# Image 0 of an eight-image kernel: two of the four directional convolutions on TensorE instead of one

## What is computed

```
def _L0_conv_ref(x, w_h, w_v, w_d45, w_d135, w_att1, w_att2, w_proj):
    feat_h = _dwconv(x, w_h, ((0, 0), (3, 3)))                 # direction 0
    feat_v = _dwconv(x, w_v, ((3, 3), (0, 0)))                 # direction 1
    feat_d45 = _dwconv(x, w_d45 * diag, ((3, 3), (3, 3)))      # direction 2
    feat_d135 = _dwconv(x, w_d135 * anti, ((3, 3), (3, 3)))    # direction 3
    feats = jnp.stack([feat_h, feat_v, feat_d45, feat_d135], axis=1)
    context = jnp.mean(feats * feats, axis=(3, 4)).reshape(x.shape[0], -1)
    hid = jax.nn.leaky_relu(context @ w_att1.T, negative_slope=0.2)
    attn = softmax over the four directions of (hid @ w_att2.T)
    feat_geom = jnp.sum(attn * feats, axis=1)
    return lax.conv_general_dilated(feat_geom, w_proj, (1, 1), ((1, 1), (1, 1)), ...)
x = x + _L0_conv_ref(_gn(x), ...)
x = x + _L1_conv_ref(_gn(x), ...)
```

## Time and profile before

| | |
|---|---|
| time of three runs | 3992.3, 3993.53, 4000.81 us; median 3993.53 |
| span of the profiled execution, first to last instruction | 4000.2 us |
| mean granted clock of TensorE | 0.963 |
| busy: PE, DVE, ACT | 93%, 76%, 41% of the span |
| L790, the start of image 0's attention | at 232.74 us |

### The profile page before, as it was taken

The page is one execution under the profiler, slowest core; times in us unless marked ns, Lnnn a source line. Parts: engine busy times, 40 slices in busy tenths (PEclk is TensorE's granted clock), DMA queues, the critical chain, the costliest instruction groups (busy, mean ns, idle before and its releaser), DMA issues.

```text
span 4000.2 us, 56479 instructions
## 1 busy us (share of the span) xinstructions
PE 3726.0 (93%) x21202; PEld 3089.2 (77%) x21202; DVE 3030.3 (76%) x2829; ACT 1624.1 (41%) x2912; POOL 210.4 (5%) x376
## 2 busy tenths in 40 slices
PE   4659999999999999999999999999999999999998
PEld 2347788968799687977889687996879778896977
DVE  7987978789777898679787897788986797853020
ACT  3412662237522564126622375225641266212430
POOL 1001000100001000010001000010000000010000
PEclk8879999999999999999999999999999999999999
DMA  4354222823156221732228221562217322260002
GB/s 111 99 148 106 64 63 43 216 63 76 35 120 171 55 67 39 175 99 64 63 44 214 63 76 37 120 169 57 66 39 177 96 65 63 46 166 27 1 7 30
DMA packets 164716, 344.11 MB, mean 86 GB/s; under 512 B 110336, under 2 KB 110576, under 8 KB 164432
## 3 DMA queue, kind: packets, MB, share of 16 engines
q1 hardware_dynamic: 141392, 255.36, 25.9%
q0 software_dynamic: 23040, 84.95, 9.6%
HBM read 189.27 MB, written 150.99 MB: 85 GB/s over the span
## 4 chain that ended last, share of the span: by engine, by line
PE 81%; DVE 10%; issue 5%; ACT 3%; DMA 1%; POOL 0%; SPq 0%; DVEq 0%; ACTq 0%; POOLq 0%
PE banks L936 15%; PE banks L937 15%; PE banks L942 15%; PE banks L951 7%; PE banks L974 6%; PE banks L1003 6%; PE banks L961 6%; DVE feat L702 5%; PE banks L1013 3%; PE banks L967 3%; PE banks L968 3%; DVE e_lo L725 2%; PE banks L990 1%; DMA feat<-feats_d 1%; ACT z L529 1%
## 5 line engine op out<-in xcount | busy, mean ns | idle before, releaser
L702 DVE SCALAR_TENSOR_TENSOR feat<-xin,w,feat 96x1536 f32<-96x1536 f32 x540 | 943.5, 1809 | 1.1
L936 PE MATMUL banks<-e_hi,a_hi 96*96 96x384 f32 x1728 | 597.6, 346 | 40.9 <-ACT a_hi L572 40.9
L936 PE MATMUL banks<-e_hi,wp_hi 96*96 96x384 f32 x1728 | 587.8, 341 | 22.5 <-DVE e_lo L828 11.5
L937 PE MATMUL banks<-e_lo,a_hi 96*96 96x384 f32 x1728 | 595.2, 345 | 0.0
L937 PE MATMUL banks<-e_lo,wp_hi 96*96 96x384 f32 x1728 | 586.8, 340 | 0.0
L702 DVE SCALAR_TENSOR_TENSOR feat<-xin,wh,feat 96x1536 f32<-96x1536 f32 x288 | 520.8, 1808 | 53.5 <-ACT feat L488 52.7
L702 DVE SCALAR_TENSOR_TENSOR feat<-xin,wv,feat 96x1536 f32<-96x1536 f32 x288 | 521.0, 1809 | 8.9 <-ACT feat L488 8.9
L500 ACT ACTIVATE sqjunk<-feat 96x1536 bf16<-96x1536 f32 x192 | 284.3, 1481 | 231.9 <-DVE feat L702 228.4
L563 ACT ACTIVATE res<-banks 96x768 f32<-96x768 f32 x96 | 77.6, 808 | 728.2 <-PE banks L942 728.2
L936 PEld LDWEIGHTS banks<-e_hi,a_hi 96*96 96x96 f32 x1728 | 287.0, 166 | 74.1 <-issue 35.0
L961 PEld LDWEIGHTS banks<-mats,z 96*96 96x96 f32 x3072 | 294.7, 168 | 60.6 <-issue 46.8
(11 more groups left out here) (145 smaller groups left out, 4844.9 us busy)
## 6 DMA issues: line engine op xcount, KB each, us to landing
feats_d<-feat SPq DMA_DIRECT2D x160, 576.0 KB, 4.1
feat<-feats_d SPq DMA_DIRECT2D x160, 576.0 KB, 6.7
feat<-in_x SPq DMA_DIRECT2D x48, 576.0 KB, 6.9
res<-in_x POOLq DMA_DIRECT2D x96, 288.0 KB, 4.0
out<-x POOLq DMA_DIRECT2D x96, 288.0 KB, 2.8
out<-res POOLq DMA_DIRECT2D x96, 288.0 KB, 4.4
xin<-in_x SPq DMA_DIRECT2D x32, 792.0 KB, 8.7
xin<-in_x SPq DMA_DIRECT2D x16, 684.0 KB, 10.3
```

The source lines that it names most:

```text
L702: dve.scalar_tensor_tensor(out=dst, in0=src, scalar=taps_w[d](k), in1=dst, op0=ALU.mult, op1=ALU.add).then_inc(tap_done, 1)
L936: pe.matmul(dst, whi[:, t, :], rows(e_hi, a0, n, dx), start=(t == CENTRE_FIRST[0]), stop=False)
L937: pe.matmul(dst, whi[:, t, :], rows(e_lo, a0, n, dx), start=False, stop=False)
```

## The change

For image 0 TensorE makes directions 1 and 3 (`BY_PE`), VectorE directions 0 and 2. A second set of seven diagonals, `v_diag`, is laid into a part of `x1` that is not yet in use, and ScalarE fills it ahead of `bk`. The semaphores `last_dir_sums` and `last_dir_made` become `pe_dir_sums` and `pe_dir_made`, which count halves of both directions in TensorE's order (`pe_halves`); the counts of VectorE's taps and ScalarE's first taps are adapted. ScalarE's order for image 0 changes: within a unit's work, the square of the second direction moves behind the normalisation and the first tap of the unit after next, and ahead of the copies out of PSUM; in `start`, both first taps come ahead of the copies. All other images are as before.

```diff
+BY_PE = (1, 3)
+def by_pe(b, d):
+    return first_image(b) and d in BY_PE
+def pe_halves(q, d):
+    return 2 * (q * len(BY_PE) + BY_PE.index(d))
...
+        v_diag = x1[0:C, 0:KT * C].rearrange("p (t c) -> p t c", c=C)
...
                 if first_image(b) and q >= 2:
-                    sp.wait_ge(last_dir_sums, 2 * (q - 1))
+                    sp.wait_ge(pe_dir_sums, pe_halves(q - 1, BY_PE[0]))
...
-                        if first_image(b) and d == DIRS - 1:
-                            sp.wait_ge(last_dir_made, 2 * (q + 1))
+                        if by_pe(b, d):
+                            sp.wait_ge(pe_dir_made, pe_halves(q, d) + 2)
...
             for k in range(KT):
+                act.activation(v_diag[:, k, :], ident, ACT.Identity, scale=wv[:, k:k + 1]).then_inc(diag_ready, 1)
+            for k in range(KT):
                 act.activation(bk[:, k, :], ident, ACT.Identity,
...
-                if by_pe:
+                if by_pe(b, d):
                     for half in range(2):
-                        act.wait_ge(last_dir_sums, 2 * q + half + 1)
+                        act.wait_ge(pe_dir_sums, pe_halves(q, d) + half + 1)
...
                 if u + 2 < UNITS:
                     work += [(first_tap, u + 2, 0), (first_tap, u + 2, 1)]
+                if first_image(b):
+                    work.append(work.pop(1))
+                    if u + 2 < UNITS:
+                        work[-2:] = work[:-3:-1]
...
-                for u in range(2):
-                    first_tap(b, u, 0)
-                    first_tap(b, u, 1)
+                order = [(0, 0), (1, 0), (0, 1), (1, 1)] if first_image(b) else [(0, 0), (0, 1), (1, 0), (1, 1)]
+                for u, d in order:
+                    first_tap(b, u, d)
...
-                    dirs = [d for d in dirs if d < DIRS - 1]
+                    dirs = [d for d in dirs if d not in BY_PE]
...
                     if first_image(b):
-                        dve.wait_ge(last_dir_sums, LEAD)
+                        dve.wait_ge(pe_dir_sums, pe_halves(LEAD // 2, BY_PE[0]))
                     edge_rows(b, NCH - 1)
...
-            def last_direction():
-                pe.wait_ge(diag_ready, KT)
+            def pe_directions():
+                pe.wait_ge(diag_ready, len(BY_PE) * KT)
                 for q in range(NCH):
                     pe.wait_ge(xin_ready, q + 1)
                     if q == 0 or q == NCH - 1:
                         pe.wait_ge(edge_zero, 1 if q == 0 else EDGES)
+                    for d, diag in zip(BY_PE, (v_diag, bk)):
+                        for half in range(2):
+                            before = pe_halves(q, d) + half - 2
+                            if before >= 0:
+                                pe.wait_ge(pe_dir_made, before + 1)
+                            for h in range(2):
+                                for k in range(KT):
+                                    dy, dx = tap_shift(d, k)
+                                    r0 = PAD + dy + (2 * half + h) * TR
+                                    last = pe.matmul(conv_ps[0:C, half, h, 0:TR * W], diag[:, k, :],
+                                                     xin[:, q % 2, r0:r0 + TR, PAD + dx:PAD + dx + W],
+                                                     start=(k == 0), stop=(k == KT - 1))
+                            last.then_inc(pe_dir_sums, 1)
```

More of the change, by code:

```diff
@@ L103, in taps_before @@
 def taps_before(b):
-    return 0 if first_image(b) else b * (NCH * TAPS) - NCH * (KT - 1)
+    return 0 if first_image(b) else b * (NCH * TAPS) - NCH * len(BY_PE) * (KT - 1)
+def by_pe(b, d):
+    return first_image(b) and d in BY_PE
+def pe_halves(q, d):
+    return 2 * (q * len(BY_PE) + BY_PE.index(d))
 def unit_taps(b, u, k, parity):
[L110 to L113, removed]
+    if first_image(b):
+        return taps_before(b) + u * (KT - 1) + k
+    return taps_before(b) + u // 2 * TAPS + u % 2 * (TAPS // 2) + 2 * (k - 1) + parity + 1
 def firsts_before(b, q):
-    return q * (DIRS - 1) if first_image(b) else b * (DIRS * NCH) - NCH + q * DIRS
+    left = DIRS - len(BY_PE)
+    return q * left if first_image(b) else b * (DIRS * NCH) - len(BY_PE) * NCH + q * DIRS
 def tap_shift(d, k):
@@ L216, in build @@
         tap_done = sem("tap_done")
-        last_dir_sums, last_dir_made = sem("last_dir_sums"), sem("last_dir_made")
+        pe_dir_sums, pe_dir_made = sem("pe_dir_sums"), sem("pe_dir_made")
         diag_ready = sem("diag_ready")
@@ L324, in load_xin @@
                 else:
-                    last_turn = TAPS - (KT - 1) if isinstance(b, int) and b == 1 else TAPS
+                    last_turn = TAPS - len(BY_PE) * (KT - 1) if isinstance(b, int) and b == 1 else TAPS
                     wait(sp, tap_done, 0 if first_image(b) else taps_before(b) + (q - 1) * last_turn)
                 if first_image(b) and q >= 2:
-                    sp.wait_ge(last_dir_sums, 2 * (q - 1))
+                    sp.wait_ge(pe_dir_sums, pe_halves(q - 1, BY_PE[0]))
                 apart(sp)
                 if isinstance(b, int) and b == 1:
-                    sp.wait_ge(last_dir_sums, 2 * NCH)
+                    sp.wait_ge(pe_dir_sums, pe_halves(NCH, BY_PE[0]))
                 if isinstance(b, int) and b == 0 and q < 2:
@@ L474, in first_tap @@
                 dy, dx = tap_shift(d, 0)
-                by_pe = first_image(b) and d == DIRS - 1
                 act.wait_ge(xin_ready, b * NCH + q + 1)
@@ L481, in first_tap @@
                     act.wait_ge(feat_stored[d], (b * (NCH - 1) + q) * 16)
-                if by_pe:
+                if by_pe(b, d):
                     for half in range(2):
-                        act.wait_ge(last_dir_sums, 2 * q + half + 1)
+                        act.wait_ge(pe_dir_sums, pe_halves(q, d) + half + 1)
                         act.activation(feat[:, d].rearrange("p (s h n) -> p s h n", s=2, h=2)[:, half],
-                                       conv_ps[0:C, half, :, 0:TR * W], ACT.Identity).then_inc(last_dir_made, 1)
+                                       conv_ps[0:C, half, :, 0:TR * W], ACT.Identity).then_inc(pe_dir_made, 1)
                     return
@@ L494, in square @@
                 d = dirs[d]
-                if first_image(b) and d == DIRS - 1:
-                    act.wait_ge(last_dir_made, 2 * (q + 1))
+                if by_pe(b, d):
+                    act.wait_ge(pe_dir_made, pe_halves(q, d) + 2)
                 else:
@@ L698, in taps @@
                     if k == 1:
-                        dve.wait_ge(tap_first, firsts_before(b, q) + d + 1)
+                        nth = d // 2 if first_image(b) else d
+                        dve.wait_ge(tap_first, firsts_before(b, q) + nth + 1)
                     else:
@@ L1053, in last_direction @@
                         pe.wait_ge(edge_zero, 1 if q == 0 else EDGES)
[L1054 to L1064, removed]
+                    for d, diag in zip(BY_PE, (v_diag, bk)):
[11 more added lines that the diff above has]
+                            last.then_inc(pe_dir_sums, 1)
             def step(b, first, second, more):
                 if first_image(b):
-                    last_direction()
+                    pe_directions()
                 def hidden():
```

## The result

The changed kernel takes 4058.07 us in the median of four runs (4053.6 to 4061.52), the kernel before 3995.02 in four on the same footing (3992.3 to 4000.81). The ratio is 1.015 with a 95% interval of 1.0138 to 1.0162: slower by 63 us. The profiled execution spans 4051.7 us. The 40 slices, and the busy shares above them, show first where the change is seen: VectorE has less to do, TensorE more, and the first slices of TensorE are fuller (compare).

A forecast was written before the change was run, and what follows sets the result against it. For image 0 VectorE set the pace before, TensorE would after: 109.86 + 156.6 + 17.5 = 284.0 us, plus a 7.35 us tail, starts the sum 58.6 us later; 3993.5 + 58.6 = 4052 us, range 4036 to 4062.

The forecast's parts named there:

- Which engine bounds: Image 0's stage before its sum: TensorE replaces VectorE as bound, 36.3 us a chunk against VectorE's 31.74 for three directions.
- The price of a record: TensorE's matmuls for image 0: 0.324 us a record at full clock, 18.14 us for a direction's 56 records.
- the fast rival: Image 0's stage: records cheap enough that VectorE stays the bound, deciding below 0.237 us each; 59 us shorter, 3935 us; 2%.
- The new wait: Between TensorE's chunks of image 0: normalisation queued behind an evacuation on ScalarE; 4.43 us three times, 4.18 once, 17.5 us.
- The cold starts: Chunks 2 to 5 on TensorE: slow clock behind each gap loses 2.9 us each; low end no loss, 10.8 us less.
- Rival (a): TensorE's gaps for image 0: the clock stays up over them; sum 47.8 us later, 4041 us; 12%.
- rival (c): Four later chunks on TensorE: low clock level holds throughout, 287 us instead of 156.6; 189 later, 4182 us; 3%.
- The tail: Behind TensorE's last matmul for image 0: last evacuation and four squares in a row before the sum, 7.35 us.
- The stage: Image 0 up to its sum: TensorE ends at 284.0 us, sum starts at 291.3 instead of 232.74, 58.6 later.
- The total: Whole kernel: median 3993.5 + 58.6 = 4052 us, 1.5% slower, since what follows the sum moves as a block.
- Edits costed at nothing: Image 0: more diagonals, VectorE's waits, the later `xin` load and PSUM halves are covered by other work, adding nothing.
- A sign that did not hold: VectorE's timeline for image 0: 72 taps with waits of 15 us and more for first taps.

The follow-up runs named there:

- e5: Changed kernel with TensorE adding only three of seven taps of directions 1 and 3 for image 0, 48 records a chunk; 3938.57 us, ratio to before 0.9850.
- e4: Changed kernel with TensorE adding only five of seven taps of directions 1 and 3 for image 0, 80 records a chunk; 3993.69 us, ratio to before 0.9994.
- e1: Changed kernel with ScalarE normalising the next chunk of image 0 ahead of the copies of direction 3 out of PSUM; 4027.5 us, ratio to before 1.0085.
- e3: Changed kernel with ScalarE's order for image 0 as in the kernel before, only the TensorE/VectorE split changed; 4061.8 us, ratio to before 1.0166.
- e2: Changed kernel with six unneeded matmuls behind each of chunks 1 to 4 of image 0, filling TensorE's gaps; 4047.97 us, ratio to before 1.0127.
- e6: Kernel before with TensorE making direction 3 and half of direction 1's rows for image 0, and normalisation ahead of the last copy; 3970.32 us, ratio 0.9935.

## Why the prediction was right, point by point

- **Which engine bounds.** TensorE took the place of VectorE, as the prices per direction said (18.14 us against 10.98). e5 shows the other side of the same point: with 48 records a chunk VectorE is the bound again.
- **The price of a record.** 0.324 us held for direction 1 to within 1%: where nothing is cold, the next block starts 18.27 us after one of direction 1 begins, against 18.14. e4 and e5 stand on the line from which the fast rival was to decide: 80 records a chunk is 5/7 of 112, as if a record cost 0.231 us, just under the 0.237 named, and the time is level with before; at 48 records the sum starts 59 us ahead of before, as the rival had it.
- **The new wait.** Predicted 4.43 us three times and 4.18 once; the trace has 4.42 and 4.18. e1 shows that it is ScalarE's order, e3 that each step in that order counts in full.
- **The cold starts.** This was the term with the widest bounds, 0 to 11 us, since no measured gap was as short. The four blocks with a cold start were taken at 84.01 us in all and measured 84.38, 10.7 us over four of 18.43; e2 takes these away and leaves the gaps. That the sum fits so closely is in part luck: single ones cost 1.8 to 3.3 us, where the working had 2.9 for each, and in e3 the same four blocks took 82.07. Rival (a), a clock that stays up, is out; the four later chunks were granted 0.92 to 0.96. So is rival (c), a low level throughout: the second block of each of these chunks takes 18.30 us, the full rate. What was said against (c), a grant of 1.00 over the first stream, was weak: the first two chunks after the change both read 1.00, though the first takes 2.4 us longer, and its weight loads stand 0.64 us apart up to 38.97 us and 0.33 us from 39.50 on. There the pace of the records shows the cold start and the granted clock does not (columns as in e2's stretches):

```profile
34.41:73.40 38.99, 38.99 (x113) 19.24 (x114) 1.00 0.20 59
73.29:109.90 36.61, 36.57 (x113) 17.92 (x111) 1.00 0.35 87
```

- **The tail.** Last copy and four squares: 291.60 - 284.26 = 7.34 us, predicted 7.35.
- **The stage.** TensorE ends at 284.26 us, predicted 284.0; the sum starts at 291.60, predicted 291.3; 58.9 us later, predicted 58.6. Two small misses cancel: TensorE started at 34.41 us instead of the 34.87 that was assumed, and the first two chunks took 75.45 us instead of 74.99.
- **The total.** 4058.07 against 4052. The interval of the ratio is worth 55 to 65 us, so the medians cannot tell 58.6 from 63. Of the 6 us, 1.5 are the median of the kernel before, which moved from 3993.53 to 3995.02 with a fourth run. The profiled executions differ by 51.5 us in span, less than the stage's 58.9, since the rest was 7.4 us shorter in the one after. That difference lies in the loop (see the last section): from one sum to the next, all six full images of the kernel before took 466.1 to 467.1 us, while four of the six after took 464.2 to 464.8. The execution traced before is the slowest of its four (4000.81), the one traced after the fastest (4053.6). Over the eight kernels, median less start of the sum lies between 3762.3 and 3766.8 us and doesn't follow that start, which points to scatter of the loop rather than an effect of the change; no run separates the two.
- **Edits costed at nothing.** VectorE's waits of 6 to 17 us for first taps, its new wait for TensorE (3.28 us ahead of the edge rows), and the later load of `xin` cost nothing: the chain runs over TensorE and ScalarE alone, in e5 the waits vanish once TensorE is ahead, and in e1 a chunk is normalised 10 us ahead of its need. With the seven more diagonals ScalarE still idles 11.46 us ahead of the first normalisation, against 14.24.
- **A sign that did not hold.** VectorE's waits for first taps were to be 15 us and more. Only one was (17.45); the other nine behind the first chunk lie between 5.57 and 13.16 us. VectorE isn't the bound, so the time doesn't depend on it.

## What to carry to other kernels

Before work is handed to an idle engine, price it there in that engine's own rows, and compare its total with the pace that the busy engine sets: TensorE was busy 123 of 191 us here, and direction 1 asked for another 109. Share by the prices, in halves if a whole is too much (e6), and let the copying engine prepare the next input ahead of the step that waits for the last output (e1). A gap on TensorE had two prices here, its length (4.2 to 4.4 us) and the slow start behind it (1.8 to 3.3 us).

## What the runs showed of the hardware

For gaps of 4.2 us and more, the price of the cold start shows no trend with the length of the gap: 1.8 to 3.3 us in one execution behind gaps of 4.2 to 4.4 us, 1.9 to 2.4 behind 6 us (e3), 2.1 to 3.1 over 18.30 behind 10 to 21 us. The gaps of 0.3 to 0.6 us that e2 leaves cost under 0.1 us. The price differs between executions at one and the same place (the first chunk's first 56 records: 20.44, 20.91, 21.56 and 21.87 us in e3, after, e2 and e1). The Trainium skill (TensorE: Matmul & The Clock Gate, "What's actually happening") calls throttling the default state, which activity releases; the trace agrees, since e2's filler matmuls, whose results nobody reads, keep the grant at 1.00.

From the start of one image's sum to the next, an image of the loop takes 463.7 to 465.2 or else 466.1 to 467.2 us, in all but 3 of the 48 full images of the eight traces. Both occur within one execution, but for the traced one of the kernel before, where all six took the longer time. Two images of e1 (length, busy time of PE, PEld, DVE, ACT and POOL with their instructions, granted clock, DMA share, GB/s); TensorE is busy 1.2 us longer in the second for the same work:

```profile
1638.52:2102.77 464.25, 447.79 (x2610) 377.41 (x2609) 385.77 (x358) 201.64 (x362) 24.58 (x45) 0.98 0.39 92
2102.77:2569.49 466.72, 449.02 (x2608) 377.09 (x2607) 385.72 (x359) 201.33 (x362) 24.59 (x45) 0.98 0.38 92
```

Which of them an image takes differs from run to run, and with some 2 us an image over six or seven images it is of the size of the scatter of the times; its cause stays open.
